# Weights, context, mask and biases laid out on the host, not turned on the chip

## The chip, the cores and the metric

The kernel runs on one core of a Trainium2 chip. The metric is the device time of one execution in microseconds; the smaller, the better. Work of the host before the launch isn't part of it.

## What is computed

A decoder layer over x [4, 1024, 256] in float32: windowed causal self attention, cross attention to a context of 77 tokens, and a gated feed-forward net with fake quantisation, each after a layer norm and added to x. Cut to what matters:

```
qkv = layernorm(x) @ w_qkv                      # 16 heads of 16; windows of 128 see themselves and the one before
x = x + softmax(mask(q k^T / 4)) v @ w_out
q = layernorm(x) @ Wq.T + bq                    # cross attention, ctx [4, 77, 256]
k = ctx @ Wk.T + bk;  v = ctx @ Wv.T + bv
scores = where(mask == 0, -inf, q k^T / 4)      # mask [1024, 77], int32
x = x + softmax(scores) v @ Wo.T + bo
h = quant(layernorm(x));  gate, up = h @ quant(w_gate).T, h @ quant(w_up).T
x = x + quant(silu(gate) * up) @ quant(w_down).T
```

## The kernel before

Attention is cut into 16 jobs (JOBS): self attention (s) or cross attention (x), batch 0 to 3, and the upper or lower eight heads (a, b). Each job has two turns g of four heads. A job projects q and k (steps "qk"), splits them into three bfloat16 parts (on ScalarE, "qk" and "split"; on VectorE the remainders), and SP moves the parts as rows into the tiles qs and ks, six rows for each head dimension ("bulk"). From these TensorE makes scores once for the maximum of each row ("max", read by VectorE's reduction at L1116 or L1120), and, with the negative maxima as three more rows (moved from tile m3t), once more for ScalarE's exponentials ("score", L912 and L916). "val" multiplies with the values (L672, L683), "out" projects and adds to x.

All engines run through one fixed list of steps. ORDER is a string of 1296 letters, each a step; every engine walks it and does its own part of each step, waiting on counting semaphores. There is no scheduler at run time: an engine that waits holds up all that is behind it in its own part of the list.

PSUM has eight banks; two hold the running sums (acc), the other six are handed out in turn to the steps that write PSUM, two at a time for steps in WIDE, one for those in NARROW. Before TensorE writes a bank it waits until the last user of that bank was read:

```
        if turn + n > of:
            turn = 0
        at[s] = (turn, [held[i] for i in range(turn, turn + n) if i in held])
```

TensorE's matmuls go through a helper, so most have the line L492; L508, L514 and L522 are transposes against an identity.

The inputs come as the reference has them. The fused weight is loaded by ScalarE's queue (L814) and copied into head order (L817, L819). The four weights of the cross attention are loaded as they are into a scratch (xwn), and eight steps "turnw" (letter W) transpose a half of one each: two transposes by TensorE (L508), then two copies by ScalarE (L831) into the right order of heads. For Wo, GpSimd first mixes the columns (step "mix", letter Z, L1405). Four steps "turnc" (K) transpose the context of one batch each (L514) and VectorE copies it out (L1037). The step "masks" (Q) makes the additive mask from the int32 one (L1045), TensorE transposes it (L522) and VectorE copies it out (L1047). wo and the biases bq and bk are fetched in head order by eight small loads (the step "late loads", L404 to L409), the biases as single elements.

In the first job "bulk" issues each part as soon as it is ready (L400 on SP's queue, and L875 on ScalarE's for the later key parts of the first turn). The feed-forward part (from about 550 us on) is a second list, not touched.

Of the kernel before, what the change touches and what calls it, by code (L numbers as in the profile page):

```python
# [7 lines left out]
BF16 = mybir.dt.bfloat16  # L8
# [9 lines left out]
KX = 77  # L18
# [16 lines left out]
    "TTzfnnnnnRnnnRNlNnnqqcAcqqcncnMCfnVnMWVmmmmDmmmmnrqmcqtmcnBqmqnLsnRAsBmCccmWMVsvmMmVWNsTmFvvsrsNZqtm"  # L35
    "mDvvvsmTmnvsesmqsvmngpvesmmcssvrsAvmnmCvmcvsntqgmqBcWscevmvVMpWmDvmWssMQeVmFAvdmrssmmgvsmKtvsmmvsnWq"
    "vmqvisesvKwccqsWmpvvnmsvCrsmecmtRqvsmsvmcssvgmmvvmseMeBVdvpKNssKLVMxrTwmvmsDsivmtNXsvvmqsgTvAmvmssvm"
    "meqsspvxvrccqsovnenmcqocnBsXntvCmonnpsosmvvgmnvssesvmdvmnRvsDwsmvMNVemvTsrNnMVtqsmvvpmmensnvsmsvvegs"
    "ATisCgBmvmvsmcmrvsdqsvtmhmpvcssmmvewsnvvAmemsmvsmssvvsvnCxhrmpsimktmmqgmBqvrvDnsgcmxsceqqvmnvcnvtsoR"
    "osecosonmvvssrvnsVsvpmvvdMmmmevssnnsemvmvmmqtrpNsgqMVtmievATsvwnCBmcesmmvvcssmvmpssemveksvNvsgmvpnsA"  # L40
    "rssvTmvgmxtmvsneivmqqsnCrcdvsRqsmtpgwvvemNscsvqsDsccvsvvdmsmBvvhMeVetrVMwvsmmTmmvssgNispevmCvmmesABx"
    "sgvmrTqpsvmtvexmvmqsccosmdosmvmemvsmssvhvrmmtwomsnipvsmvemhmgsqnhscvrqhmmAqsvnvsCogeccxsvqvnBvtcpsou"
    "rsVosvDMuedpVMtsvmnvegnvmsyknosmysvvmmsmemivmwsnRrqNvecqmAvBocptsvmmsmvmssmmveesTyNmrvvsgTysvsyitqqs"
    "veCskxdvvssvmwmvycgsemspvACcsmvgvpsmvstsvveBrkyhmvvmemxsysgsrsdptvimvmmwuvemevrqqCgYussAsmvsmvxvmccd"
    "vtehmeoonnonipsnrsonnhntsnBsRwhvmmmveANvgpCmgNBssTsevTrxqqccpodwtomoUgosmyvvuvvemmkeshysprtysP1svmyk"
    "vgimmquysvsveesmhrCcsvvutveuvAhdmxyqesycs2mysmYmpsvvhwitgvrveh22km3B4mmsmxses4r44v4o45t4oy4o5y5osp4m"
    "v554memmeryiUuvvu5styysspsv5yeyuvvye5Y5vg5sssseue44v4vvvd455p5ibbxxUogyyowgjyyojypyojyyJYjJJJ6E5")
# [7 lines left out]
def streams():  # L55
# [45 lines left out]
        "W": [("turnw", i, c) for i in range(4) for c in range(2)],  # L101
        "K": [("turnc", b) for b in range(NB)],
# [7 lines left out]
        "Z": [("mix",)],  # L110
# [25 lines left out]
NARROW = {"turnw", "turnc", "masks", "keys", "qk", "v", "xkeys", "turnm", "out", "broad", "wturn", "turnx", "down", "dsc", "peak"}  # L136
# [19 lines left out]
def build(nc, x_in, ctx_in, mask_in, w_qkv, w_out, Wq, bq, Wk, bk, Wv, bv, Wo, bo, clip_x, clip_d, w_gate, w_up,  # L156
          w_down, out):
    with ExitStack() as ctx:
# [71 lines left out]
        ctxn = oT["x"][0][:, 0:NB * D].rearrange("p (b d) -> p b d", b=NB)  # L230
        xwn = xnT[1][:].rearrange("p a b -> p (a b)").rearrange("p (w c d) -> p w c d", w=4, c=2)
        wo_mixed = oc[:, 0:512].rearrange("p (c n) -> p c n", c=2)
        maskn = oTx[:, 0:NC * KX].bitcast(I32).rearrange("p (c k) -> p c k", c=NC)
        wqkvn = big[:, 16384:17920].rearrange("p (c n) -> p c n", c=2)
# [31 lines left out]
        def wq_of(job, z):  # L266
# [20 lines left out]
        p_set, p_ones, p_mix, p_rstd, p_rstd3, p_one, p_sel, p_shift, p_pick, p_wend = (  # L287
            sem("p_" + n) for n in ("set", "ones", "mix", "rstd", "rstd3", "one", "sel", "shift", "pick", "wend"))
        a_wqkv, a_turnw, a_keys, a_xnT, a_p0, a_p1, a_v, a_m3t, a_exp, a_evac, a_wb, a_wT, a_centre = (
            sem("a_" + n) for n in ("wqkv", "turnw", "keys", "xnT", "p0", "p1", "v", "m3t", "exp", "evac", "wb", "wT",  # L290
                                    "centre"))
        d_set, d_ones, d_ctx, d_mask, d_keys, d_clear, d_stat, d_ve, d_xn, d_rem, d_p2, d_xv, d_max, d_rows, d_inv, d_scale = (
            sem("d_" + n) for n in ("set", "ones", "ctx", "mask", "keys", "clear", "stat", "ve", "xn", "rem", "p2", "xv", "max",
# [4 lines left out]
        t_turnw, t_ctx, t_mask, t_keys, t_norm, t_qk, t_v, t_xv, t_max, t_turnm, t_score, t_val, t_out, t_w = (  # L298
            sem("t_" + n) for n in ("turnw", "ctx", "mask", "keys", "norm", "qk", "v", "xv", "max", "turnm", "score",
# [20 lines left out]
        def read_out(s):  # L320

            k, n = s[0], n_of[s]
            if k in ("turned",):
                return a_xnT, 2 * n
            if k == "wturn":
                return a_wT, w_done(s)
            if k == "broad":
                return d_scale, len(JOBS) + s[1]
            return {"turnw": a_turnw, "turnc": d_ctx, "masks": d_mask, "keys": a_keys, "qk": d_rem, "v": a_v,
                    "xkeys": d_xv, "max": d_max, "turnm": a_m3t, "score": a_exp, "out": d_out}[k], {  # L330
                        "turnw": 2 * n, "masks": 2 * n, "keys": 3 * n - 2, "xkeys": 2 * n}.get(k, n)
# [43 lines left out]
        def run_sync(e):  # L375
# [12 lines left out]
            for s in plan:  # L388
# [13 lines left out]
                elif k == "late loads":  # L402
                    for c in range(2):
# [1113 lines left out]
```

## Time and profile before

| | |
|---|---|
| median of 3 runs | 686.54 us |
| runs | 683.77, 686.54, 692.66 us |
| profiled execution | 687.23 us |
| its span | 685.4 us |
| granted TensorE clock, mean | 0.962 |
| TensorE busy | 611.8 us, 89% |
| VectorE busy | 515.5 us, 75% |
| ScalarE busy | 405.4 us, 59% |
| GpSimd busy | 168.2 us, 25% |

The span runs from the first to the last instruction; the execution's own time has 1.8 us more. Busy shares are means over stages of unlike limits. Times in the rows below are from the span's start.

### The profile page before, as it was taken

Reading aid. Unit: us, or ns where it says so; the run is one execution under the profiler, and the core shown is the slowest. Engines: PE = TensorE matmul, PEld = TensorE weight load, DVE = VectorE, ACT = ScalarE, POOL = GpSimd, SP = SyncE. Lnnn points to the kernel's source line nnn. Section 1 sums busy time; section 2 is a strip of 40 time slices with the busy share of each in tenths; the row PEclk is TensorE's granted clock in tenths of the full one; section 3 lists DMA queues with packets and bytes.
Section 4 is the critical chain, followed back from the end, with each engine's and each line's share of the span. In section 5 each row is a group of like instructions: output and inputs, shape, how many; then the busy total and the mean of one; then the engine's idle time right before and its main releaser. Section 6 shows DMA issues by size and latency. Waiting matters only on the chain.

```text
span 685.4 us, 19992 instructions
## 1 busy us (share of the span) xinstructions
PE 611.8 (89%) x8024; PEld 395.9 (58%) x8024; DVE 515.5 (75%) x983; ACT 405.4 (59%) x602; POOL 168.2 (25%) x216
## 2 busy tenths in 40 slices
PE   2799999999998999999999999999989984888484
PEld 2557575866765776566758655576656642333263
DVE  6698777777887677648766865787687587699987
ACT  3335666775675547565554576545364654899691
POOL 2004332421343211330251024112102011455300
PEclk9899999999999999999999999999997987899798
DMA  7644233562344344247323373533464330000024
GB/s 258 183 151 144 50 116 112 147 153 66 113 133 118 98 124 102 70 127 180 107 57 126 96 156 104 116 77 99 111 197 107 67 64 0 0 1 1 0 93 154
DMA packets 58266, 71.61 MB, mean 104 GB/s; under 512 B 23819, under 2 KB 35263, under 8 KB 58175
## 3 DMA queue, kind: packets, MB, share of 16 engines
q1 hardware_dynamic: 54495, 68.36, 36.0%
q10 hardware_dynamic: 3680, 1.97, 1.1%
q8 instruction: 65, 1.06, 0.7%
q14 instruction: 26, 0.21, 0.1%
HBM read 17.21 MB, written 4.69 MB: 32 GB/s over the span
## 4 chain that ended last, share of the span: by engine, by line
PE 64%; DVE 15%; issue 5%; ACT 5%; DMA 5%; SPq 4%; ACTq 0%; POOL 0%; DVEq 0%
PE banks L492 41%; PE banks L672 8%; PE banks L592 5%; PE banks L683 3%; DVE mtop L1116 3%; PE banks L536 2%; PE banks L741 2%; SPq L425 2%; DVE tops L1323 2%; DMA out_dram<-oTs 1%; DVE mtop L1120 1%; ACT xnT L992 1%; PE banks L595 1%; SPq L443 1%; SPq L420 1%
## 5 line engine op out<-in xcount | busy, mean ns | idle before, releaser
L492 PE MATMUL banks<-big 96*128 96x77 bf16 (+3 forms) x1348 | 162.9, 242 | 8.2 <-DMA big<-kparts 3.2
L1116 DVE TENSOR_REDUCE mtop<-banks 128x4 f32<-128x640 f32 (+3 forms) x128 | 127.2, 1019 | 40.9 <-PE banks L601 40.4
L492 PEld LDWEIGHTS banks<-big 99*128 99x128 bf16 (+2 forms) x1348 | 104.7, 103 | 76.1 <-issue 36.8
L1424 POOL TENSOR_SCALAR_AFFINE_SELECT big<-big 128x512 f32<-128x512 f32 x96 | 65.3, 680 | 228.9 <-ACT big L912 228.0
L912 ACT ACTIVATE big<-banks 128x1024 f32<-128x1024 f32 x96 | 96.9, 1028 | 37.7 <-PE banks L492 37.4
L492 PE MATMUL banks<-xnT,weights 128*128 128x512 f32 x192 | 91.3, 605 | 0.2 <-DVE mtop L1116 0.2
L592 PE MATMUL banks<-big 96*32 96x160 bf16 (+3 forms) x1792 | 71.2, 258 | 0.5 <-DVE mtop L1116 0.2
L916 ACT ACTIVATE big<-banks 77x1024 f32<-77x1024 f32 x48 | 47.8, 1022 | 29.4 <-PE banks L492 27.2
L1120 DVE TENSOR_REDUCE mtop<-banks 128x8 f32<-128x616 f32 x64 | 49.3, 790 | 19.7 <-PE banks L492 19.5
L672 PE MATMUL banks<-big 128*17 128x256 f32 x768 | 57.0, 382 | 0.0
L925 ACT COPY oe<-banks 128x512 f32<-128x512 f32 x64 | 36.6, 588 | 32.2 <-DMA oTx<-oe 11.7
L741 PE MATMUL banks<-oe,weights 128*128 128x512 bf16 x192 | 47.4, 394 | 9.2 <-ACT oe L981 5.1
L601 PE MATMUL banks<-causal,identb 128*32 128x64 bf16 x1024 | 53.3, 196 | 0.0
L492 PEld LDWEIGHTS banks<-xnT,weights 128*128 128x128 f32 x192 | 33.6, 190 | 31.2 <-issue 27.8
L492 PE MATMUL banks<-maskt,identb 77*77 77x512 bf16 x128 | 49.1, 384 | 0.0
L592 PEld LDWEIGHTS banks<-big 96*32 96x32 bf16 x1792 | 39.7, 98 | 10.5 <-DVE mtop L1116 3.8
L869 ACT CAST parts<-banks 128x512 bf16<-128x512 f32 x32 | 18.7, 586 | 41.5 <-PE banks L492 29.1
L595 PE MATMUL banks<-big 96*32 96x128 bf16 x256 | 34.8, 224 | 6.8 <-DMA big<-parts 5.6
L1095 DVE TENSOR_TENSOR parts<-big,parts 128x512 bf16<-128x512 f32 x48 | 33.3, 705 | 9.3 <-ACT parts L879 8.9
L1470 POOL TENSOR_TENSOR big<-xn,xnT 128x512 f32<-128x512 f32 x24 | 30.7, 1280 | 37.7 <-ACT xn L999 37.7
L492 PE MATMUL banks<-maskq,identb 128*128 128x308 bf16 x128 | 38.4, 306 | 0.0
L741 PEld LDWEIGHTS banks<-oe,weights 128*128 128x128 bf16 x192 | 17.9, 100 | 35.1 <-ACT oe L981 8.8
(168 smaller groups left out, 1187.8 us busy)
## 6 DMA issues: line engine op xcount, KB each, us to landing
big<-parts SPq DMA_DIRECT2D x285, 128.0 KB, 2.5
oc<-sums SPq DMA_DIRECT2D x15, 512.0 KB, 4.7
oTs<-oe SPq DMA_DIRECT2D x64, 64.0 KB, 2.7
out_dram<-oTs SPq DMA_DIRECT2D x16, 256.0 KB, 2.2
xs<-in_x_dram SPq DMA_DIRECT2D x3, 1024.0 KB, 6.3
big<-oe SPq DMA_DIRECT2D x32, 64.0 KB, 2.4
oTx<-oe SPq DMA_DIRECT2D x32, 64.0 KB, 2.3
xs<-in_x_dram SPq DMA_DIRECT2D x2, 512.0 KB, 6.4
```

Source lines behind the costliest of these rows:

```text
L492: return e.matmul(to[0:w], k[:, 0:w], q, start=start, stop=stop, skip_group_check=True)
L592: e.matmul(to, q, K[0:96, hh, k0 - 128:k0 + own], start=(i == 0), stop=False, tile_position=(0, 32 * u), skip_group_check=True)
L595: e.matmul(to[:, 0:128], q, K[0:96, hh, 0:1].to_broadcast([96, 128]), start=(i == 0), stop=False, tile_position=(0, 0), skip_group_check=True)
L601: t = e.matmul(bank(p, j)[32 * u:32 * u + 32, :].rearrange("p (s n) -> p s n", s=2)[:, :, 96 + own:128 + own], identb[:, 32 * u:32 * u + 3 ...
L672: t = e.matmul(acc[:, col // 512][32 * i:32 * i + 17, col % 512:col % 512 + z - a], va[f][:, j, 4 * g + i, :], P[:, i, a:z], start=new, st ...
L741: t = e.matmul(bank(p, z), wguT[:, z, i, t0 * 128:t0 * 128 + 128], xqT[blk % 2][:, i, :], start=(i == 0), stop=(i == 1))
L912: e.activation(pt[u].rearrange("p (i n) -> p i n", i=4)[:, :, 0:n], pair(p).rearrange("p j (s n) -> p (j s) n", s=2)[:, :, 0:n], ACT.Exp, ...
L916: e.activation(pt[u][0:KX, :].rearrange("p (s n) -> p s n", s=2), pair(p)[0:KX], ACT.Exp, scale=SCALE).then_inc(a_exp, 1)
L925: e.copy(oe[:, half * 512:half * 512 + 512], acc[:, half]).then_inc(a_evac, 1)
L1116: e.tensor_reduce(M.rearrange("p (h c) -> p h c", h=4)[:, :, c], pair(p).rearrange("p j (s n) -> p (j s) n", s=2)[:, :, 0:160 + 32 * (c % 4)],
L1120: e.tensor_reduce(M.rearrange("p (h c) -> p c h", h=4)[:, c:c + 2, :], pair(p)[:, :, 0:4 * KX].rearrange("p j (s n) -> p j s n", s=4), AX. ...
L1424: e.affine_select(out=P[:, :, 0:128], in_=P[:, :, 0:128], compare_op=ALU.is_ge, fill=0.0, base=0, pattern=[[0, 4], [1, 128]], channel_mult ...
```

## The change

The host lays out the inputs (function laid_out): the fused weight and wo with the heads inside, the four cross attention weights transposed and in head order as one array, the context transposed, the mask both ways, the biases as one array of four columns. The kernel loads each straight into the tile where it is used. The letters W (eight), K (four) and Z (one) are gone from ORDER; the other 1283 letters keep their sequence. The step "masks" stays, without its transposes: a second load brings the transposed mask, and VectorE makes the additive form of both. It takes no bank any more, nor do the removed steps, so the hand-out of banks shifts behind them. The late loads become two. Waits on the removed steps go or become waits on the loads.

```diff
-NARROW = {"turnw", "turnc", "masks", "keys", "qk", "v", "xkeys", "turnm", "out", "broad", "wturn", "turnx", "down", "dsc", "peak"}
+NARROW = {"keys", "qk", "v", "xkeys", "turnm", "out", "broad", "wturn", "turnx", "down", "dsc", "peak"}
...
-        "W": [("turnw", i, c) for i in range(4) for c in range(2)],
-        "K": [("turnc", b) for b in range(NB)],
...
-        "Z": [("mix",)],
...
+        masktn = oT["x"][0][0:KX, :].bitcast(I32)
...
-            for i, w in enumerate((Wk, Wv, Wq, Wo)):
-                e.dma_start(xwn[:, i], w.rearrange("(c p) n -> p c n", p=128)).then_inc(ld_xw, 16)
-            e.dma_start(ctxn[0:KX], ctx_in.rearrange("b k d -> k b d")).then_inc(ld_ctx, 16)
-            e.dma_start(maskn, mask_in.rearrange("(c p) k -> p c k", p=128)).then_inc(ld_mask, 16)
+            for i in range(4):
+                e.dma_start(xw[:, i], xw_in[:, i]).then_inc(ld_xw, 16)
+            e.dma_start(ctxT, ctx_in).then_inc(ld_ctx, 16)
+            e.dma_start(maskn, mask_in).then_inc(ld_mask, 16)
+            e.dma_start(masktn, maskt_in).then_inc(ld_mask, 16)
...
                 elif k == "late loads":
-                    for c in range(2):
-                        e.dma_start(wo[:, c, :], w_out[c * 128:c * 128 + 128, :].rearrange("(h d) n -> d h n", d=HD)
-                                    ).then_inc(ld_wo, 16)
-                        e.dma_start(bias[:, 2 + c:3 + c], bk[c * 128:c * 128 + 128].rearrange("(h d a) -> d h a", d=HD, a=1),
-                                    allow_slow_non_contiguous=True).then_inc(ld_bias, 16)
-                        for g in range(2):
-                            e.dma_start(bias[64 * g:64 * g + 64, c:c + 1],
-                                        bq[c * 128 + 64 * g:c * 128 + 64 * g + 64].rearrange("(h d a) -> d h a", d=HD, a=1),
-                                        allow_slow_non_contiguous=True).then_inc(ld_bias, 16)
+                    e.dma_start(wo, wo_in).then_inc(ld_wo, 16)
+                    e.dma_start(bias[:], bias_in).then_inc(ld_bias, 16)
...
                 elif k == "keys":
                     f = s[1]
-                    e.wait_ge(a_turnw, 16)
-                    e.wait_ge(d_ctx, NB)
+                    e.wait_ge(ld_xw, 64)
+                    e.wait_ge(ld_ctx, 16)
...
         def run_scalar(e):
-            e.dma_start(wqkvn, w_qkv.rearrange("(c p) n -> p c n", p=128)).then_inc(ld_wqkv, 16)
-            e.wait_ge(ld_wqkv, 16)
-            for i in range(2):
-                e.copy(wqkv[:, i, 0:512].rearrange("p (f d h) -> p f h d", f=8, h=4),
-                       wqkvn[:, i, 0:512].rearrange("p (f h d) -> p f h d", f=8, h=4)).then_inc(a_wqkv, 1)
-            e.copy(wqkv[:, :, 512:768], wqkvn[:, :, 512:768]).then_inc(a_wqkv, 1)
+            e.dma_start(wqkv, wqkv_in).then_inc(ld_wqkv, 16)
...
                 elif k == "masks":
-                    e.wait_ge(ld_mask, 16)
+                    e.wait_ge(ld_mask, 32)
                     e.tensor_scalar(maskq[:], maskn, 0.0, NEG, ALU.is_equal, ALU.mult).then_inc(d_mask, 1)
-                    e.wait_ge(t_mask, 1)
-                    e.tensor_copy(maskt[0:KX, :], bank(p).bitcast(BF16)[0:KX, :]).then_inc(d_mask, 1)
+                    e.tensor_scalar(maskt[0:KX, :], masktn, 0.0, NEG, ALU.is_equal, ALU.mult).then_inc(d_mask, 1)
...
+def laid_out(np, given):
+    a = {}
+    def by_p(w):
+        return w.reshape(2, 128, w.shape[1]).transpose(1, 0, 2)
+    def heads_inside(w, h):
+        n = w.shape[-1] // (16 * h)
+        return w.reshape(w.shape[:-1] + (n, h, 16)).swapaxes(-1, -2).reshape(w.shape)
+    a["ctx"] = given["ctx_1024"].transpose(2, 0, 1).reshape(2, 128, NB * KX).transpose(1, 0, 2)
+    a["mask"] = given["mask_SxS2_ik0"].reshape(NC, 128, KX).transpose(1, 0, 2)
+    a["maskt"] = given["mask_SxS2_ik0"].T
+    qkv = given["L0_attn_w_qkv"]
+    a["wqkv"] = by_p(np.concatenate([heads_inside(qkv[:, 0:512], 4), qkv[:, 512:768]], axis=1))
+    a["wo"] = by_p(heads_inside(given["L0_attn_w_out"].T, 8).T)
+    wk, wv, wq, wx = (given["L0_xattn_" + n].T for n in ("Wk", "Wv", "Wq", "Wo"))
+    a["xw"] = np.stack([by_p(heads_inside(wk, 8)), by_p(wv), by_p(heads_inside(wq, 4)),
+                        by_p(heads_inside(wx.T, 8).T)], axis=1)
```

## Rows read from the trace of the kernel before

**Rows 1.** The page: busy time and share, then the chain's shares by engine

```profile
PE 611.8 (89%) x8024; PEld 395.9 (58%) x8024; DVE 515.5 (75%) x983; ACT 405.4 (59%) x602; POOL 168.2 (25%) x216
...
PE 64%; DVE 15%; issue 5%; ACT 5%; DMA 5%; SPq 4%; ACTq 0%; POOL 0%; DVEq 0%
```

**Rows 2.** Stretches: length, PE, PEld, DVE, ACT, POOL busy, clock, DMA share

```profile
60.00:100.00 40.00, 39.06 (x818) 26.13 (x818) 31.42 (x54) 26.00 (x42) 15.03 (x20) 1.00 0.28 84
```

**Rows 3.** The chain that ended last, 0 to 60 us: start, length, what

```profile
0.81 5.93 DMA xs<-in_x_dram
...
16.24 6.88 PE banks L492 x16
...
26.79 4.46 DMA big<-parts
...
32.49 7.57 DVE mtop L1116 x8
```

**Rows 4.** SP's queue in order of time, 0 to 38 us

```profile
8.13 0.37 SPq L379 DMA_DIRECT2D xs<-in_x_dram  x1
...
16.37 0.67 SPq L404 DMA_DIRECT2D weights<-in_L_attn_w_out_dram  x1
...
20.91 0.59 SPq L409 DMA_DIRECT2D bias<-in_L_xattn_bq_dram  x1
21.54 15.04 SPq L400 DMA_DIRECT2D big<-parts  x21
```

**Rows 5.** Timeline of the other engines, 19 to 32 us

```profile
19.71 0.59 ACT L869 CAST parts<-banks 128x512 bf16<-128x512 f32 x1 [1.13 <-PE banks L492]
...
25.13 2.02 ACTq L875 DMA_DIRECT2D big<-parts  x3
...
31.61 0.26 PE L595 MATMUL banks<-big 96*32 96x128 bf16 x1 [4.71 <-DMA big<-parts]
```

**Rows 6.** DMA issues, 0 to 46 us: count, KB each, median us to landing

```profile
big<-parts SPq DMA_DIRECT2D x21, 128.0 KB, 2.7
...
big<-in_L_attn_w_qkv_dram ACTq DMA_DIRECT2D x1, 768.0 KB, 5.6
```

**Rows 7.** The chain that ended last, 41 to 135 us, pieces of turning steps

```profile
50.46 0.43 PE banks L508 x2
...
56.54 0.22 PE banks L508 x2
...
91.76 0.45 PE banks L522 x8
...
99.43 0.35 PE banks L514 x2
```

**Rows 8.** Groups by line and shape, whole span

```profile
L831 ACT COPY weights<-banks 128x128 f32<-128x128 f32 x16 | 4.3, 350 | 0.0
...
L1045 DVE TENSOR_SCALAR maskq<-oTx 128x616 bf16<-128x616 int32 x1 | 0.5, 471 | 0.0
```

**Rows 9.** Timeline, 48 to 104 us, around steps whose bank's last user changes

```profile
48.46 1.95 ACT L912 ACTIVATE big<-banks 128x1024 f32<-128x1024 f32 x2
...
49.95 0.31 PE L592 MATMUL banks<-big 96*32 96x160 bf16 x8
...
57.38 1.05 ACT L912 ACTIVATE fourth<-banks 128x1024 f32<-128x1024 f32 x1
58.02 0.40 PE L592 MATMUL banks<-big 96*32 96x256 bf16 x8
...
94.72 1.96 DVE L1116 TENSOR_REDUCE mtop<-banks 128x4 f32<-128x1024 f32 x2 [1.78 <-PE banks L601]
...
95.42 1.21 PE L492 MATMUL banks<-big 99*128 99x256 bf16 x12
...
100.99 1.02 ACT L912 ACTIVATE big<-banks 128x1024 f32<-128x1024 f32 x1 [0.85 <-PE banks L492]
...
101.22 0.34 PE L592 MATMUL banks<-big 96*32 96x192 bf16 x8
```

**Rows 10.** Stretches of 2 us, columns as in rows 2

```profile
30.00:32.00 2.00, 0.39 (x19) 0.42 (x23) 0.18 (x1) 0.00 (x0) 0.00 (x0) 0.50 0.81 257
```

More of the change, by code:

```diff
@@ L34 @@
 ORDER = (
[L35 to L44, printed above, removed]
@@ L286, in build @@
         land_y = [sem(f"land_y{i}") for i in range(4)]
[L287 to L290, printed above, removed]
+        p_set, p_ones, p_rstd, p_rstd3, p_one, p_sel, p_shift, p_pick, p_wend = (
+            sem("p_" + n) for n in ("set", "ones", "rstd", "rstd3", "one", "sel", "shift", "pick", "wend"))
+        a_keys, a_xnT, a_p0, a_p1, a_v, a_m3t, a_exp, a_evac, a_wb, a_wT, a_centre = (
+            sem("a_" + n) for n in ("keys", "xnT", "p0", "p1", "v", "m3t", "exp", "evac", "wb", "wT",
                                     "centre"))
-        d_set, d_ones, d_ctx, d_mask, d_keys, d_clear, d_stat, d_ve, d_xn, d_rem, d_p2, d_xv, d_max, d_rows, d_inv, d_scale = (
-            sem("d_" + n) for n in ("set", "ones", "ctx", "mask", "keys", "clear", "stat", "ve", "xn", "rem", "p2", "xv", "max",
+        d_set, d_ones, d_mask, d_keys, d_clear, d_stat, d_ve, d_xn, d_rem, d_p2, d_xv, d_max, d_rows, d_inv, d_scale = (
+            sem("d_" + n) for n in ("set", "ones", "mask", "keys", "clear", "stat", "ve", "xn", "rem", "p2", "xv", "max",
                                     "rows", "inv", "scale"))
@@ L297, in build @@
             sem("d_" + n) for n in ("out", "stat3", "ve3", "top3", "end3", "ctr", "far", "wtop", "wsc", "w8"))
-        t_turnw, t_ctx, t_mask, t_keys, t_norm, t_qk, t_v, t_xv, t_max, t_turnm, t_score, t_val, t_out, t_w = (
-            sem("t_" + n) for n in ("turnw", "ctx", "mask", "keys", "norm", "qk", "v", "xv", "max", "turnm", "score",
+        t_keys, t_norm, t_qk, t_v, t_xv, t_max, t_turnm, t_score, t_val, t_out, t_w = (
+            sem("t_" + n) for n in ("keys", "norm", "qk", "v", "xv", "max", "turnm", "score",
                                     "val", "out", "w"))
@@ L328, in read_out @@
                 return d_scale, len(JOBS) + s[1]
-            return {"turnw": a_turnw, "turnc": d_ctx, "masks": d_mask, "keys": a_keys, "qk": d_rem, "v": a_v,
+            return {"keys": a_keys, "qk": d_rem, "v": a_v,
                     "xkeys": d_xv, "max": d_max, "turnm": a_m3t, "score": a_exp, "out": d_out}[k], {
-                        "turnw": 2 * n, "masks": 2 * n, "keys": 3 * n - 2, "xkeys": 2 * n}.get(k, n)
+                        "keys": 3 * n - 2, "xkeys": 2 * n}.get(k, n)
         def w_done(s):
@@ L823, in run_scalar @@
                     p = at_bank[s][0]
[L824 to L833 removed]
+                if k == "keys":
                     f, n = s[1], NB * KX
                     e.wait_ge(t_keys, n_of[s])
[L836 removed]
+                    e.wait_ge(ld_bias, 16)
                     if f:
                         e.wait_ge(d_keys, 2)
[L839 to L840 removed]
                     e.activation(kf[:, 0:n], bank(p)[:, 0:n], ACT.Identity, bias=bias[:, 2 + f:3 + f]).then_inc(a_keys, 1)
@@ L1397, in run_gpsimd @@
                 e.memset(va[f][:, :, :, 16:17], 1.0).then_inc(p_set, 1)
-            pool_steps = [s for s in plan if s[0] in ("ones", "mix", "root", "xkeys", "shift", "root3", "pick", "wend")
+            pool_steps = [s for s in plan if s[0] in ("ones", "root", "xkeys", "shift", "root3", "pick", "wend")
                           or (s[0] == "score" and s[1][0] == "s")]
@@ L1508 @@
     arrays, args = {}, []
-    for name in _INS:
-        a = _np.ascontiguousarray(inputs[name])
+    for name, a in laid_out(_np, {n: _np.asarray(v) for n, v in inputs.items()}).items():
+        a = _np.ascontiguousarray(a)
         arrays[f"in_{name}_dram"] = a
```

100 lines of the change are left out of this document (28 added, 72 removed).

## The prediction

> **What bounds the kernel now.** I read the busy shares and the shares of the chain first: TensorE is busy for 89% of the span, and 64% of the chain that ended last is TensorE's [rows 1]. The table of stretches says where that holds: from 60 to 100 us TensorE is busy for 39.06 of 40 us at full granted clock [rows 2], and so on to about 550 us. There, TensorE work that goes is time that goes, unless the wait for a bank's reader takes its place. The start is another regime, and the chain is to be read there in order of time [rows 3]: first half of x (lands at 6.74), normalisation, TensorE's projections of the first job back to back (16.24 to 23.12), then a DMA of the six-part rows on SP's queue (26.79 to 31.26, issued by L400), and then VectorE, whose eight maxima of 7.57 us in all set the pace. TensorE stands idle for 4.7 us before 31.61 [rows 5]. So the start is set by DMAs and VectorE, and the change touches the queue that issues those DMAs.
>
> **The change part by part.** ScalarE's three copies of the fused weight go, and so do the first two weight transposes (the first W of ORDER, at 24.7 us). I cost both at nothing: the copies run before 9 us, while TensorE has nothing before normalised x, and the transposes are covered by the idle time before 31.61. If that cover were gone, two transposes would be worth 0.4 us.
>
> Late loads. Before its first row DMA, SP issues eight small loads (two for wo, two for bk, four for bq), back to back from 16.37 to 21.50; L400 follows at 21.54 [rows 4]. The first part that it moves was ready when ScalarE's second cast ended, at 19.71 + 0.59 = 20.30 [rows 5]. With two loads in place of eight at the 0.6 us an issue of these rows, and one added mask load of 0.6 us ahead of them, SP is free at 16.37 + 0.6 + 1.2 = 18.2, so the cast now releases it: a start at about 20.35, 1.2 us earlier. From there SP issues 21 DMAs in 15.04 us, 0.72 us each, without a real gap, so the whole train moves by 1.2 us, both the piece that ends at 31.26 and the last one, on which the second half of the heads waits near 40.5. Bounds: the other parts of the same keys go through ScalarE's queue, which ends its issues at 25.13 + 2.02 = 27.15 [rows 5] because it waits for VectorE's last split, and that end doesn't move. With the median landing of 2.7 us [rows 6], counted from an issue that begins near 26.5, they are there at 29.2, so the gain is at most 2.0 us; at least it is nothing, if the key parts of ScalarE's queue already land with SP's. I take 1.2, since the queue's own shift is the nearest thing measured. Less idle time ahead of the first maxima may also spare TensorE the 1.2 GHz level that it has from 30 to 36 us (granted 0.50, three rows alike) [rows 10]; only the 0.9 us from 31.61 to VectorE's first maximum depends on it, so 0 to 0.4 us, and I take 0.
>
> TensorE steps on the chain. From 41 us on I go down the chain in order of time and add up what belongs to lines that go [rows 7]: six pieces of weight transposes (L508: one of 0.43, five of 0.22 like the one shown) make 1.53; four of the context (L514: 0.35, two of 0.28, one of 0.13) make 1.04; the mask's eight transposes (L522) 0.45. That is 3.0 us. One more pair, at 90.1 us, lies beside a VectorE maximum that sets the time there, and counts nothing.
>
> Other engines. ScalarE loses 16 copies of 0.35 us, 5.6 us of work of which 4.3 shows as busy [rows 8]; they sit between exponentials and never on the chain, so directly they give nothing, and at best they bring some exponentials forward, for which I allow 1 us in the lower bound. GpSimd loses one copy at 63 us and VectorE four context copies, neither on the chain. The transposed mask is now computed by a second VectorE operation: priced by elements from the first one (0.471 us for 616 per partition [rows 8]) 1024 come to 0.78 us, in place of a copy of the same tile and a wait for TensorE. VectorE then waits for TensorE before its next maximum anyway, so 0. Loads with longer runs move the same bytes behind idle SP time: 0. The waits that are added (matmuls of keys and values on the loads of weights and context, at 130 us and later) find loads that have been there for 100 us.
>
> Banks. This is what the change moves without naming it. Steps that write PSUM take the six banks in turn, and twelve turning steps and the mask step leave the sequence. I counted banks_of over the two ORDER strings: apart from the removed letters the order is the same; the 554 common steps keep their bank in 422 cases, and from plan place 313 on (near 150 us) they are all the same. Before that, eleven steps now get a bank whose last user is only two bank steps back, where it was a transpose or an earlier step. TensorE then waits for that user's reader. With the times of the trace before [rows 9]:
> - The fifth maximum of the first job's second half of heads (starts 49.95) needs the second exponential, which ends at 48.46 + 1.95 = 50.41: 0.5 us. The one ahead of it, 0.1 us.
> - The eighth one (58.02) needs the exponential that ends at 57.38 + 1.05 = 58.43: 0.4 us.
> - Two scores that run from 95.42 need the two maxima that end at 96.68; the second, two thirds of the 1.21 us, can then start at 96.7 and not at 95.8. TensorE's next step waited until 96.73, so 0.6 us of it shows.
> - A maximum at 101.22 needs the exponential that ends at 100.99 + 1.02 = 102.01: 0.8 us.
> - The five others find the reader done or within 0.1 us.
>
> Together 2.4 us. The bounds are 0 (the freed ScalarE time brings those exponentials forward) and eleven times a whole reader of about 1.0 us, 11 us. I take 2.4, since it rests on each case's own rows.
>
> Sum: −1.2 (SP's train) − 3.0 (TensorE) + 2.4 (banks) = −1.8 us. The profiled execution took 687.23 us (span 685.4 and 1.8 around it), so it would take 685.4. The median of the runs, 686.54, is 0.7 below the profiled one: 684.7.
>
> **What late x would cost.** Both halves of x and the fused weight are loaded at once, the weight on ScalarE's queue (768 KB, 5.6 us to landing [rows 6]), x on SP's. Before, the weight has runs of 3 KB in DRAM and x of 1 KB; after, the weight's are 6 KB. If that gives the weight's queue a greater share, x lands later and the whole chain behind it with it. The first half can't be later than the second is now, which is at most 8.13 [rows 4] against 6.74, so 1.4 us. I take 0: the weight had landed before x already, so x has little left to yield. The Trainium skill speaks for this danger: "DMA: Bandwidth & Descriptors", section "Queues, rings and completion order", says that each DMA engine takes turns between the queues that have work, one packet at a time. By that rule the larger pieces of the weight would push x back towards that bound; the trace before shows one layout only, and so can't say.
>
> **Rivals.**
> - *Banks cost more than they are thought to* (slower). Place: the eleven steps between 49 and 145 us. Price: if each waits for a whole reader, 11 us, so 687.23 − 1.2 − 3.0 + 11 = 694.0, median 693.3. It decides the sign once the added waits pass 4.2 us. For it: the trace has TensorE waiting for VectorE's maxima already. Against: in most cases the reader was nearly done by its own row.
> - *Late x.* 687.23 + 1.4 − 3.0 + 2.4 = 688.0, median 687.3. Against: the bytes stay the same.
> - *The time comes back as waits.* VectorE's maxima and ScalarE's exponentials keep their pace in 50 to 145 us, and only SP's 1.2 us stay: 686.0, median 685.3. For it: on the chain between the TensorE pieces stand short pieces of maxima.
> - *More than the sum.* No bank wait, exponentials 1 us sooner, SP's train by 2.0: −6.0, 681.2, median 680.5. This would take every bound at its best end.
> - *The change doesn't do what it says*: the steps are gone from ORDER, so only their price is open.
>
> **How the numbers follow.** The forecast with its near neighbours (−0.5 to −4 us) gets 0.48, the time that comes back 0.20, late x 0.08, dear banks 0.12, more than the sum 0.12. The range goes from 679 (a little under the best case, since three runs of one kernel lie 683.77 to 692.66 apart) to 691 (half of the dear-bank case). About 2%, or 13.7 us, is what a measurement of this kernel can tell from no change. Only unpriced things could reach that, such as a timing that tips over far down the fixed order: faster by over 2% 0.03, slower 0.02, within 0.95.
>
> **What would show it.** In the profile after: SP's L400 train starts near 20.3 instead of 21.5; the DMA piece of the chain ends near 30.1 instead of 31.3; VectorE's eight maxima start near 31.3. The chain has no transposes of weights, context or mask. TensorE idles before the fifth and eighth maximum of the second half for some tenths, released by the exponentials, and once near 100 us for 0.8. From 150 us on the two traces should be the same up to a constant of about 1.8 us. A first half of x that lands after 7.0, a sum of new waits for L912 and L1116 above 4 us before 150 us, or an offset that grows after 150 us would prove me wrong.

## The result, and the profile after

The kernel after takes 693.28 us (median of 22 runs, 686.08 to 701.65), the kernel before in the same session 687.39 us (22 runs, 683.77 to 694.12). The ratio of the two is 1.006, interval [1.0042, 1.0078]: slower, though by less than the 2% that a single measurement can tell. The ratio leaves out executions more than 1.5% above the fastest of their kernel (5 of 22 of after), so the medians (1.0086) lie further apart than the ratio. The profiled execution of after took 693.2 us, with a span of 691.5.

The forecast was 684.7 in 679 to 691. It was wrong in direction and in range.

The page of after, the busy lines and the chain's shares, to be set beside [rows 1]; the middle line is of the list of DMA queues (packets, MB, share):

```profile
PE 611.2 (88%) x7987; PEld 394.7 (57%) x7992; DVE 515.5 (75%) x979; ACT 398.5 (58%) x583; POOL 165.5 (24%) x215
...
q8 instruction: 64, 1.05, 0.7%
...
PE 56%; DVE 15%; SPq 9%; ACT 6%; issue 6%; DMA 6%; ACTq 1%; POOL 0%; DVEq 0%
```

Work went as the diff says: ScalarE 6.9 us less, GpSimd 2.7 less, VectorE the same. The busy times say that no work became dearer, so the loss has to be looked for in idle time and in the clock. To find its place I matched each VectorE and ScalarE instruction of the one trace with the same one of the other and took the difference of their ends, after less before. The medians by stretch of before's time:

| stretch, us | 20-40 | 60-80 | 100-120 | 120-140 | 160-180 | 240-260 | 380-400 | 480-500 | 620-640 |
|---|---|---|---|---|---|---|---|---|---|
| after less before | +0.2 | -0.4 | -0.3 | -0.8 | +4.4 | +6.2 | +6.0 | +8.2 | +7.6 |

Up to 145 us the change gains, a little less than was forecast. Between 145 and 150 us 5.0 us are lost at once. Two smaller steps follow, near 214 us (1.8) and near 470 us (1.6).

**The early part.** SP's queue in order of time, after (beside [rows 4]); two loads stand where eight stood, and the row train starts at 20.56, not 21.54:

```profile
14.55 0.51 SPq L399 DMA_DIRECT2D weights<-in_wo_dram  x1
15.10 0.45 SPq L400 DMA_DIRECT2D bias<-in_bias_dram  x1
20.56 14.47 SPq L396 DMA_DIRECT2D big<-parts  x21
```

The chain in order of time, 24 to 60 us, after (beside [rows 3]): the DMA piece ends at 30.76 (before 31.25) and the eight maxima start at 32.00 (before 32.49):

```profile
26.74 4.02 DMA big<-parts
30.76 0.35 issue
31.11 0.27 PE banks L556
...
32.00 7.56 DVE mtop L1052 x8
```

**The step at 145 us.** The chain of after, 143 to 154 us: start, length, what. L553 is the matmul of a maximum, L592 before.

```profile
144.86 0.03 PE banks L562 x4
144.89 0.20 PE banks L553 x6
145.09 3.05 issue
148.14 0.21 PE banks L553
...
148.71 4.47 PE banks L479 x12
```

The timeline of TensorE in after: in brackets stands the idle time before the instruction, and what ended it.

```profile
144.71 0.39 PE L553 MATMUL banks<-big 96*32 96x256 bf16 x6
148.14 0.29 PE L553 MATMUL banks<-big 96*32 96x256 bf16 x2 [3.05 <-issue]
148.15 0.21 PE L562 MATMUL banks<-causal,identb 128*32 128x64 bf16 x2
```

This is the row to dwell on. TensorE stops between the sixth and the seventh of eight equal matmuls of one step. The code has no wait there, and the profile names no releaser: "issue" means that the engine waited for nothing that the trace shows. What it lacked, as the rest of this section argues, were the instructions themselves. The list of queues shows where these come from. The DMA traffic of after by queue in three stretches, 134 to 145, 145 to 147 and 147 to 148.5 us (packets, MB, share):

```profile
q1 hardware_dynamic: 1603, 2.09, 70.6%
q10 hardware_dynamic: 99, 0.02, 1.0%
...
q1 hardware_dynamic: 270, 0.47, 102.3%
q8 instruction: 1, 0.02, 4.0%
...
q1 hardware_dynamic: 159, 0.25, 73.2%
```

and of before, 137 to 139 and 139 to 148 us:

```profile
q1 hardware_dynamic: 77, 0.14, 38.0%
q10 hardware_dynamic: 99, 0.02, 5.5%
q8 instruction: 1, 0.02, 4.0%
...
q1 hardware_dynamic: 1486, 2.10, 88.8%
```

q8 carries 64 packets in the whole execution, 1.05 MB, so 16 KB each; 7987 matmuls and 7992 weight loads over 64 packets are 250 recorded TensorE instructions to a packet. I read these packets as TensorE's code, fetched during the run; the stops below bear it out. The Trainium skill, page "Advanced Engine Details and Errata", section "ISA Cache", gives a line as 16 KB or 256 instructions and says that there are only two of them, though it also gives 128 KB as TensorE's size, which would be eight. The trace agrees with the size of a line by its packets, and with two lines rather than eight, since TensorE stopped after some 460 recorded instructions, waits not counted (below). In after one fetch starts at 133.1 and the next at 145.5: TensorE passed 231 matmuls and 229 weight loads between them, nearly two packets' worth, and ran dry. In before there is a fetch at 137.4, in a stretch with a DMA share of 0.48, and the next at 148.7; 212 and 205 instructions lie between them, and the engine did not stop. That was close: by 1.3 us after the end of that later packet before had passed 449. The cause of the delay that I argue for, and test below, is the traffic of SP's queue: x's last 1 MB load, a 512 KB broadcast and six 128 KB row DMAs, issued from 137.85 to 143.44. The stretches of after and of before (length; busy PE, PEld, DVE, ACT, POOL; granted clock; DMA share; GB/s):

```profile
142.00:145.00 3.00, 2.99 (x86) 1.77 (x77) 1.85 (x3) 1.91 (x4) 0.83 (x2) 1.00 1.00 271
145.00:148.00 3.00, 0.10 (x3) 0.00 (x0) 1.03 (x1) 0.47 (x1) 0.63 (x1) 1.00 1.01 232
148.00:151.00 3.00, 2.86 (x22) 1.33 (x22) 1.23 (x1) 0.00 (x0) 0.00 (x0) 0.76 0.11 31
151.00:154.00 3.00, 3.00 (x26) 1.50 (x25) 1.77 (x3) 2.12 (x3) 0.38 (x1) 0.68 0.03 8
```

```profile
142.00:145.00 3.00, 3.00 (x88) 2.02 (x87) 1.78 (x2) 2.11 (x5) 0.86 (x2) 1.00 1.05 316
145.00:148.00 3.00, 3.00 (x56) 1.79 (x48) 2.22 (x2) 1.13 (x3) 1.05 (x2) 1.00 1.04 239
148.00:151.00 3.00, 3.00 (x27) 1.55 (x26) 2.37 (x6) 3.00 (x5) 1.38 (x2) 1.00 0.54 116
```

The burst is in both kernels, at the same place and size. Only after has PE at 0.10 of 3.00 us in it. Then the second half of the loss: behind the stop the granted clock falls to 0.50, the 1.2 GHz level. The means of 0.76 and 0.68 over two stretches of 3 us are (0.24 + 0.32) x 3 / 0.5 = 3.4 us at half speed, which costs 1.7 us. With the 3.05 us of the stop that is 4.75 of the 5.0 us.

**The two later steps.** Near 214 us a DMA of key parts is waited for, and SP's queue is on the chain ahead of it. An issue of L414 there takes 1.91 us instead of 0.60 (`207.83 1.91 SPq L414`), with a q8 fetch inside it at 207.7; TensorE then idles and the clock falls again (after, same columns):

```profile
214.00:217.00 3.00, 0.60 (x15) 0.48 (x11) 1.10 (x5) 0.61 (x1) 2.75 (x3) 1.00 0.11 19
217.00:220.00 3.00, 3.00 (x32) 2.75 (x30) 2.41 (x5) 1.29 (x2) 0.78 (x3) 0.63 0.59 199
```

Near 470 us a wait of 1.41 us for VectorE's maximum is followed by a clock of 0.50 in 474 to 477 us, where before had a like gap without the fall. I did not test these two. The second profile of after (below) has no such steps of over 1 us there, so the change does not bring them each time.

### The profile page after: what moved, and what is told of

It is laid out like the page before. It is cut to its first block, busy times and chain, and to the rows that moved or that the text cites. A ratio compares the mean times of both kernels' runs of the same rounds, so it can differ in the third digit from the quotient of the medians.

```text
span 691.5 us, 19893 instructions
## 1 busy us (share of the span) xinstructions
PE 611.2 (88%) x7987; PEld 394.7 (57%) x7992; DVE 515.5 (75%) x979; ACT 398.5 (58%) x583; POOL 165.5 (24%) x215
## 3 DMA queue, kind: packets, MB, share of 16 engines
q8 instruction: 64, 1.05, 0.7%
## 4 chain that ended last, share of the span: by engine, by line
PE 56%; DVE 15%; SPq 9%; ACT 6%; issue 6%; DMA 6%; ACTq 1%; POOL 0%; DVEq 0%
PE banks L479 36%; PE banks L633 6%; SPq L414 4%; PE banks L553 4%; DVE mtop L1052 3%; PE banks L644 3%; SPq L432 2%; PE banks L499 2%; DVE tops L1259 2%; PE banks L702 2%; SPq L409 2%; DMA oc<-sums 1%; ACT xnT L934 1%; ACT big L854 1%; DMA oTx<-oe 1%
## 5 line engine op out<-in xcount | busy, mean ns | idle before, releaser
L553 PE MATMUL banks<-big 96*32 96x160 bf16 (+3 forms) x1792 | 72.1, 259 | 5.0 <-issue 3.0
L553 PEld LDWEIGHTS banks<-big 96*32 96x32 bf16 x1792 | 40.2, 98 | 15.7 <-issue 6.4
```

What stands on the lines that cost most here:

```text
L553: e.matmul(to, q, K[0:96, hh, k0 - 128:k0 + own], start=(i == 0), stop=False, tile_position=(0, 32 * u), skip_group_check=True)
```

## The experiments

The theory, called F in the expectations: the change takes 32 transposes, 64 TensorE instructions with their weight loads, out of the stream ahead of 145 us. That moves every later code fetch, and one of them now falls into the burst, comes late, and TensorE runs dry and loses its clock. Rivals: the new hand-out of banks; the removed instructions as such; many small accidents.

All twelve, with the kernel before beside each (its median was 687.37 in the first session, 686.33 in the second, 686.56 in the third). The last column counts the executions over 690 us; before had 4 of 22 beside after, then 3 of 34 (an execution of 2065 us is left out), 0 of 35 and 0 of 23.

| kernel | median, us | runs from - to | ratio to before | over 690 |
|---|---|---|---|---|
| after | 693.28 | 686.1 - 701.7 | 1.0060 [1.0042, 1.0078] | 16 of 22 |
| after, 32 tiny matmuls | 690.16 | 683.4 - 693.9 | 1.0029 [0.9998, 1.0060] | 7 of 12 |
| after, banks of before | 689.62 | 684.2 - 693.7 | 1.0032 [1.0005, 1.0058] | 4 of 12 |
| after, 128 tiny matmuls | 691.97 | 687.9 - 702.9 | 1.0057 [1.0029, 1.0084] | 10 of 12 |
| after, late load | 688.97 | 683.2 - 694.3 | 0.9998 [0.9970, 1.0025] | 3 of 12 |
| after, banks of before, late load | 685.95 | 682.9 - 692.8 | 1.0008 [0.9981, 1.0035] | 1 of 12 |
| before, late load | 686.38 | 682.6 - 688.9 | 1.0000 [0.9981, 1.0019] | 0 of 12 |
| before, 96 tiny matmuls | 692.85 | 683.7 - 696.6 | 1.0046 [1.0012, 1.0080] | 8 of 12 |
| after, 32 tiny matmuls, late load | 688.58 | 684.9 - 694.0 | 1.0024 [0.9999, 1.0048] | 2 of 12 |
| before, 128 tiny matmuls | 688.70 | 685.9 - 690.8 | 1.0029 [1.0006, 1.0053] | 2 of 12 |
| before, 96 tiny matmuls, late load | 688.40 | 684.5 - 693.3 | 1.0024 [0.9996, 1.0052] | 2 of 12 |
| after, second profile | 690.40 | one run | | |
| before, 96 tiny matmuls, second profile | 694.49 | one run | | |

**Give the instructions back (e1_pad32).** 32 matmuls of one column, with their weight loads 64 instructions, ahead of the first maximum, where TensorE is idle:

```diff
 elif k == "max":
     ...
+    if n_of[s] == 1:
+        e.wait_ge(d_set, 1)
+        for _ in range(32):
+            e.matmul(bank(p)[0:32, 0:1], identb[:, 0:32], identb[:, 0:1], start=True, stop=True,
+                     tile_position=(0, 0), skip_group_check=True)
```

> The changed kernel with 32 small bfloat16 matmuls (64 TensorE instructions) more, put in front of the first maximum, where TensorE idles for about 4 us; they write a bank that is overwritten at once. Theory F (TensorE's instruction fetch): the change took some 64 TensorE instructions out of the first 145 us, so each 16 KB fetch stands 64 instructions earlier in the list than before, and one falls into the burst of x's last load at 138 to 146 us. With 64 instructions back, the fetches stand as before: no stall of 3 us near 145 us, and the profile 4 to 6 us under the changed kernel's 693.2, near 687 to 688. Theory B (banks, whose last user is closer): nothing changes, 693. A third, that the row DMAs themselves land late behind x's load: nothing changes, 693.

Measured 690.16. The trace has no stop at 145 us (fetches at 140.6 and 151.1), and the offset to before stays at 2.1 to 2.3 us from 120 to 180 us. But it was already 1.9 at 60 us, part of it since x landed late in this one execution (chain: `0.81 6.59 DMA xs<-in_x_dram`, beside 5.88 to 6.13 in all other traces but one of 6.71). The jump goes in this trace; the median recovers by 3.1 of 5.9 us, no more, 7 of 12 executions stay over 690, and the interval of its ratio overlaps that of after. So this run alone doesn't prove the part of the instruction count.

**The banks of before (e2_banks).** ORDER of before, with W, K and Z as steps that issue nothing and only take a place in the turn of banks:

```diff
+        "W": [("gone", i) for i in range(8)],
+        "K": [("gone", i) for i in range(8, 12)],
+        "Z": [("nothing",)],
...
-        n = WIDE.get(s[0], 1 if s[0] in NARROW else 0)
+        empty = s[0] in ("gone", "masks")
+        n = WIDE.get(s[0], 1 if s[0] in NARROW or empty else 0)
...
+        if empty:
+            turn += 1
+            continue
```

> The changed kernel with the hand-out of banks of the kernel before: the removed steps and the mask step still count a bank each, and nothing is written in it. Theory B: the waits for near readers before 150 us go, 2 to 5 us less than the changed kernel, 688 to 691. Theory F: the fetches stand where they stood, so the stall near 145 us stays, and only what the trace shows as bank waits before 140 us goes, at most 1 us: 692 to 693.5.

Measured 689.62. The two kernels part where the forecast put the waits. The timeline of TensorE in after, 46 to 60 us, its first bank waits:

```profile
49.61 0.32 PE L553 MATMUL banks<-big 96*32 96x160 bf16 x8 [0.38 <-ACT big L854]
57.63 0.40 PE L553 MATMUL banks<-big 96*32 96x256 bf16 x8 [0.34 <-ACT fourth L854]
```

And from 90 to 104 us the other two:

```profile
94.56 1.34 PE L479 MATMUL banks<-big 99*128 99x256 bf16 x12 [0.61 <-DVE mtop L1052]
101.12 0.35 PE L553 MATMUL banks<-big 96*32 96x192 bf16 x8 [0.64 <-ACT big L854]
```

None of the four is in the trace with the banks of before. At 120 to 140 us that trace is 2.2 us ahead of before and after's is 0.8 ahead (at 100 to 120 us 2.4 and 0.3), so the banks cost 1.4 to 2.1 us, beside a forecast of 2.4. They are not the loss at 145 us, for the stop is there all the same. The chain with the banks of before, 143 to 151 us:

```profile
143.56 0.10 PE banks L561 x3
143.67 2.68 issue
146.35 0.43 PE banks L561 x5
```

Its instruction stream is that of after. The offset goes from -2.2 to +2.5 there, 4.7 us.

**A whole packet more (e3_pad128).** The same pad with 128 matmuls, 256 instructions.

> As the run with 32 small matmuls, with 128 of them, 256 instructions. A fetch of 16 KB comes once in about 256 instructions in both traces. Theory F with that period: the fetches stand where they stand in the changed kernel, so the stall near 145 us is back, 693, plus what the matmuls cost if they outlast the idle time (0 to 2 us). If the 32 matmuls helped only by keeping TensorE busy in the idle time, 128 help at least as much: 688 or less.

Measured 691.97, with after's long tail (to 702.9, 10 of 12 over 690). The profiled execution, 690.87, has no stop at 145 us; it has one at 127.9 (`127.91 1.44 issue`) beside a fetch that came 428 instructions after the last. So the times repeat those of after, the place in this one trace does not: where a fetch falls is not fixed by the count alone. Its interval overlaps that of the run with 32, so the two lengths are not told apart by the ratio.

**Take the burst away (e4_late_x3).** The letter L of x's last load moves down the list; SP issues it at 158.04 us, not at 137.85. TensorE's instructions stay as in after.

```diff
-    "wccqsm...eBVdvpNssLVMxrTwmvmsDsivmtNXsvvmqsgTvAmvmssvm..."
+    "wccqsm...eBVdvpNssVMxrTwmvmsDsivmtNXsvvmqsgTvALmvmssvm..."
```

> The changed kernel with the load of x's last batch (1 MB, issued at 138 us) moved down SP's list behind the next row DMAs, to about 162 us, where the DMA engines have little to do; its data are read at about 190 us. Theory F: TensorE's fetch at 139 to 145 us finds free DMA engines, no stall and no stretch at 1.2 GHz there: 4.5 to 5.5 us less than the changed kernel, 688. A new fetch may meet the moved load at 162 to 168 us, then less is gained. Theory B: nothing changes, 693.

Measured 688.97, ratio 0.9998: 4.3 us under after, and the one repair whose interval (up to 1.0025) lies clear of that of after (from 1.0042). The instruction stream is the same, so the fetches can be set side by side: after's start at 133.1 and 145.5, these at 133.5, 139.1 and 146.0. Without x's load the second one came some 6 us sooner. Stretches of its trace: the first still has a DMA share of 1.04, the next 0.25, and TensorE does not stop in them:

```profile
142.00:145.00 3.00, 2.99 (x88) 1.81 (x84) 1.79 (x2) 1.91 (x5) 0.83 (x2) 1.00 1.04 221
145.00:148.00 3.00, 3.00 (x59) 1.79 (x48) 2.22 (x2) 1.13 (x3) 1.08 (x2) 1.00 0.25 59
```

**The same move in before (f2_before_late).**

> The kernel before, with x's last load moved down the list to the same place as in the run with the late load. Theory F: before had no stall at this load, so moving it is worth nothing there: within 0.5 us of before, 686.9 to 687.9. Rival (the late load is a gain for any kernel, since the burst slows other transfers too, and e4's 4.3 us isn't the stall's): 2 to 4 us faster than before.

Measured 686.38 against 686.33. The move is worth nothing by itself; so what it brought in after is what after had lost at that place.

**Both repairs (f1_banks_late).**

> The kernel after with both repairs: the banks handed out as in the kernel before, and x's last load moved down SP's list to about 162 us. Theory F (instruction fetch of TensorE inside the burst of loads at 145 us costs 4 to 5 us with the clock stretch behind it; the new bank order costs 1.5 to 2 us): the two gains add, since each was measured alone (-4.3 us and -3.7 us against the kernel after, the second partly by luck of phase): no stall at 145 us, 0 to 1 clock stretch at 0.5 between 37 and 514 us, offset against before about -2.5 us at 120 to 200 us, and a time 1.5 to 3 us under before (684.5 to 686 where before is 687.4). Rival G (the spread of this kernel comes from many small accidents, one repair only moves them): a time within 1 us of before, stalls over 1 us at new places.

Measured 685.95 against 686.33, ratio 1.0008. This missed: the theory wanted 1.5 to 3 us under before. The rival written beside it, that small accidents only move, wanted a time within 1 us of before and idle times over 1 us at new places, and both came. The stop at 145 us is gone, but the chain has this:

```profile
210.18 5.33 PE banks L487 x53
215.51 1.42 issue
```

It is of another kind: the next instruction waits for semaphores, and no fetch starts between 211.5 and 222.7 us. The kernel with only the banks of before has 1.14 us of it at 218.4. The trace is 1.0 us ahead of before from 120 to 180 us and 0.8 ahead at 620 us. The trace with the banks alone was 2.2 ahead at 120 us; 0.9 us of the difference are there by 40 us, where the two kernels are the same, so single traces can differ by that much from the start. Set against the late load alone, which has the other banks, it gains 2.1 us between 50 and 130 us, once more the price of the banks. Beside after, timed in another session, the repairs restored the time of before, and no version beat before by what the measurement can tell.

**Put the fault into before (f3_before_pad96).** 96 of the tiny matmuls, 192 instructions; with the 64 that before has more than after that is 256, one packet. So before's fetches should fall as after's.

> The kernel before with 96 tiny matmuls (192 TensorE instructions) ahead of its first maximum; with the 64 instructions that the change removes these make 256, the number between two instruction fetches, so that its fetches fall as in the kernel after. Theory F: the stall at about 145 us appears in the kernel before, 2 to 3 us long, with the clock at half for 3.4 us behind it, and the time is 3 to 6 us above before (690.5 to 693.5), 1 us of it the pad's own. Rival (the phase of the fetches hangs on more than the count, or the cause is another part of the change): no stall, only the pad's own cost of about 1 us, 688 to 688.8.

Measured 692.85, 6.5 us over before, with 8 of 12 executions over 690 where before had none of 35. But the profiled execution was one of the short ones (687.75), without a stop at 145 us.

**Its second profile (g4_pad96_again).**

> The kernel before with 96 tiny matmuls, for a second profile. Its times are spread from 683.7 to 696.6 us and the first profile fell on a fast one (687.8). Theory F: if this execution takes over 690 us, its trace shows a stop of TensorE of 1.5 us or more beside a late fetch between 120 and 220 us, which the trace of before has not. Rival: the loss is spread over the whole span, with no stop.

Measured 694.49. Its chain, 145 to 151 us:

```profile
146.40 0.21 PE banks L597 x6
146.61 2.63 issue
149.24 0.21 PE banks L597
```

The stop is at the same matmul of the same step as in after, the seventh of the same eight, in a kernel that has no other part of the change. The offset goes from +0.9 to +5.5 there, 4.5 us before rounding. Between the fetches at 134.4 and 146.7 lie 239 matmuls and 236 weight loads.

**After once more (g3_after_again).**

> The kernel after, unchanged, for a second profile. Theory F: an execution of 690 us or more shows a stop of TensorE of 1.5 us or more beside a late instruction fetch (at 143 to 150 us most likely); one under 688 us shows none there. Rival (the stop in the first profile was a chance event): a slow execution without such a stop.

Measured 690.40. Chain, 145 to 150 us; again behind the sixth matmul:

```profile
145.38 0.21 PE banks L553 x6
145.59 3.31 issue
148.91 0.21 PE banks L553
```

The offset goes from -0.3 to +5.2, 5.5 us. So the loss at 145 us alone is nearly all that the medians differ by.

**A whole packet more in before (g1_before_pad128).** More padding than the 96, but a full turn.

> The kernel before with 128 tiny matmuls (256 instructions, a whole period) ahead of its first maximum, beside 192 in the run with 96. Theory F (what matters is where the fetches fall, not how many instructions are added): the fetches of the middle of the kernel are back where before has them, and only the pad's own price of 0.5 to 1.5 us is left: a median of 687 to 688.3 where before is 686.5 to 687.4, and the spread of before (6 us) and not of the run with 96 (13 us). Rival (the pad itself costs, in proportion to its length): 692 to 695, more than with 96 matmuls.

Measured 688.70, 4.2 us under the kernel with fewer matmuls added, 2 of 12 over 690 where that one had 8 of 12. The loss does not grow with the pad, as the rival wanted. By the ratios, though, 1.0029 and 1.0046, the two are not apart, for their intervals overlap; that the loss goes again with a whole packet rests on the count of long executions and on one trace, with a fetch at 139.4, as before has at 137.4, and no stop at 145 us. What is left over before is 2.1 us, more than I had allowed for the pad. The trace has 1.5 us of it from 60 to 180 us, in an execution in which x landed 0.8 us late, and 0.2 at 620 us.

**96 matmuls and the late load (g2_before_pad96_late).**

> The kernel before with 96 tiny matmuls, which alone made it 692.9 us, and x's last load moved down SP's list to about 162 us, which alone changed nothing (686.4 to 686.3). Theory F: the load is the other half of the clash, so it goes: 687 to 689. Rival (the slow executions of the run with 96 come from another place of the clash, or from the pad): 691 to 694 as without the move.

Measured 688.40: by the medians 4.5 us come back by the move that was worth nothing in before, though here too the intervals of the ratios (1.0024 and 1.0046) overlap. The profiled execution was 693.3 all the same. It has a stop of 1.11 us at 126.1, one at 147.8, and a loss of 4 us at 320 us, behind which the granted clock was 0.50 for 6.8 us.

```profile
147.60 0.21 PE banks L597 x6
147.81 0.98 issue
148.79 0.21 PE banks L597
```

That is the seventh of the same eight matmuls again, without x's load: a fetch at 135.6 was followed by the next at 146.0, with the broadcast and the row DMAs as the traffic. So moving the load shortens the clash and need not end it.

**Pad and late load in after (f4_pad32_late).**

> The kernel after with 32 tiny matmuls and the late load together. Theory F: both remove the same stall, so they don't add: 688 to 690, that is the late load's time (689.0 in the first batch, -0.2 against before) plus the pad's own price of 0.5 to 1 us. Rival (each removes a loss of its own): they add, and the time is 3 us under that of the late load alone, about 686.

Measured 688.58. They do not add, as two cures of one fault shouldn't, though 2 us of pad price would hide a small sum.

**All the stops side by side.** In the fourteen traces there are eleven stops of over 0.5 us between equal matmuls of one step, where nothing is waited for: five from 143 to 149 us (3.05, 3.31, 2.63, 2.68 and 0.98 us) and six of 0.58 to 1.44 us near 125 us, where the traffic is row DMAs and a broadcast. Each begins 454 to 495 recorded instructions after the start of the fetch before the late one, and in each TensorE goes on 1.3 to 1.6 us after the late q8 packet has ended. This is the best evidence that the fetch is the releaser that the profile doesn't name. No trace has more than 511 recorded instructions between the start of a fetch and 1.3 us after the end of the next.

The offsets to before of the main traces, as worked out above:

| stretch, us | 60-80 | 100-120 | 120-140 | 160-180 | 380-400 | 620-640 |
|---|---|---|---|---|---|---|
| after | -0.4 | -0.3 | -0.8 | +4.4 | +6.0 | +7.6 |
| after, second profile | +0.1 | +0.1 | -0.3 | +5.2 | +5.5 | +4.6 |
| after, banks of before | -1.1 | -2.4 | -2.2 | +2.5 | +1.9 | +3.7 |
| after, late load | -0.7 | -0.6 | -0.2 | 0.0 | -0.8 | -0.4 |
| after, both | -0.2 | -1.5 | -1.1 | -1.0 | -1.2 | -0.8 |
| before, 96 matmuls, second profile | -0.1 | -0.1 | +0.9 | +5.5 | +5.1 | +8.2 |
| before, 128 matmuls | +1.5 | +1.5 | +1.5 | +1.5 | +0.3 | +0.2 |

## Why the prediction was wrong

**The step that failed** is in "How the numbers follow" and "What would show it": that from 150 us on the two traces would be the same up to a constant of about 1.8 us, since from there the banks and the list are the same. The offset was +4.4 us from 160 us on and +7.6 at 620. The sum had no term for what was lost just ahead of that place, at 145 us. The prediction costed what the removed instructions do as work, as bank users and as loads on SP's queue. It did not cost that they are also bytes of code, which TensorE fetches through the DMA engines that move the data. The count of instructions stood in [rows 1], and the page of before has a line for q8, 65 packets, that I never asked about. "A timing that tips over far down the fixed order" stood there as an unpriced thing, put at nothing in the sum and given a chance of 0.02 to cost over 2%; its real size was 5 us, and it should have widened the range upward to 694 or more. The dear-bank rival gave 693.3, nearly the measured 693.28, but for a cause that the runs refute: that is luck.

Point by point:

- *SP's train 1.2 us earlier.* It started at 20.56 instead of a forecast 20.35, 1.0 us earlier than before; the first DMA piece of the chain and the maxima were 0.5 us earlier, at 30.76 and 32.00, and not 1.2; by 50 us the offset was -0.9. Right in mechanism, 0.3 too large.
- *TensorE pieces, 3.0 us.* Mis-sized by half. With the banks of before the offset goes from -0.9 at 50 us to -2.4 or -2.5 by 120 us: 1.6 us; with both repairs from 0.0 to -1.5. The first piece shows why. The chain of before gives the pair of transposes 0.43 us and what follows 2.23:

```profile
50.46 0.43 PE banks L508 x2
50.90 2.23 PE banks L492 x20
```

and the kernel with the banks of before but no transposes has

```profile
49.54 2.48 PE banks L487 x20
```

so 2.66 us became 2.48, a gain of 0.18 and not of 0.43. Matmuls overlap on TensorE (in the timeline of before eight of L592 run from 142.33 to 142.65 and the four of L601 start at 142.47); a piece of the chain ends where the next one starts, and part of its length is the other's. The chance for "the time comes back as waits" was too low, but this isn't that rival: nothing else took over.
- *Banks, 2.4 us.* Measured 1.4 to 2.1, at the places named: 0.38, 0.34, 0.61 and 0.64 us for a forecast of 0.5, 0.4, 0.6 and 0.8. A count over the list and the rows of each case was enough, and "dear banks" is refuted.
- *Late x.* 0.14 us in the profiled execution (6.07 us against 5.93). Over all traces the piece is 5.95 to 6.13 us long in seven of after's kind and 5.88 to 5.98 in five of before's, with one straggler in each (6.59 and 6.71). So x lands about 0.1 us later behind the larger pieces of the weight, far from the bound of 1.4.
- *Sum until 145 us.* Forecast -1.8, measured -0.6 to -0.8. The sign was right there.
- *From 145 us.* +5.0 us, of them 3.05 the stop and 1.7 the half clock. Not foreseen.

What is shown, and what stays open. Shown by changing one side at a time: most of the loss needs the burst (it goes with the late load, which is worth nothing where there is no loss), and more instructions ahead of it can bring the loss into the kernel before (192 of them: 8 of 12 executions over 690, none of 35 without, and the same stop in the trace). That it is their phase, the place at which the fetches fall, and not their number is made likely, not shown, by its going again with 256. Open is why a fetch comes late in one execution and not in the next: the trace shows when a packet moves, not when it was asked for, and the kernel before with 96 matmuls spreads over 13 us. Open too are the pad's own price, and why the kernel with the banks of before, stop and all, runs 3.7 us under after by the medians when the banks explain 1.4 to 2.1 (the intervals of the two ratios overlap). And without stop and dear banks the change still brought nothing that could be measured (685.95 against 686.33).

## What to carry to other kernels

Instructions are data. In this kernel of 16 thousand TensorE instructions on a fixed schedule the code came in 64 packets of 16 KB, by the same DMA engines as the loads, and adding or removing some can move every later fetch against the bulk DMAs. A stop with the releaser "issue" in the middle of a step that has no wait is the sign, and the instruction queues in the list of DMA traffic are where to look; the same word ahead of an instruction that does wait can mean something else. Before trusting a gain or a loss of 1% on such a kernel, shift the phase with a pad of idle instructions, or move the burst, and time again. And a piece of the chain isn't what its removal brings: compare the span of its neighbours with and without it.

## What the runs showed of the hardware

- TensorE ran dry after 460 (after), 464 (after again) and 475 (before with 96 matmuls) recorded matmuls and weight loads since the start of the last fetch; 417 passed in before without a stop. The stop lasted 2.6 to 3.3 us, and it fell on the same matmul in these three executions, and for 0.98 us in a fourth (before with 96 matmuls and the late load).
- In eleven stops TensorE went on 1.3 to 1.6 us after the end of the late 16 KB packet, which itself took 1.0 to 1.4 us.
- A stop of 3.05 us with a DMA share of 1.01 was followed by 3.4 us at 1.2 GHz; so were those of 2.63 and 3.31 us (granted clock 0.50 and 0.53 in 151 to 154 us) and the one of 2.68 us with the banks of before. No such fall stands behind the seven of 0.58 to 1.44 us.
- An issue on SP's queue that coincides with one of TensorE's code fetches can take over 1 us instead of 0.6 (1.91 at 207.83 us of after). Of 29 issues of over 1 us in after 28 overlap a fetch, of 34 in before 31; 40 and 45 shorter ones overlap one too, so it is a risk and not a rule.
- 128 matmuls of one column in TensorE's idle time at 27 us (they take 3.40 us, with 1.71 us of idle time left behind them) still made the kernel before slower, by 2.1 us (1.0029, interval [1.0006, 1.0053]); why isn't shown.
